# Cross-attention of a decoder layer: the context's layer norm folded into the key and value weights, the context loaded turned

## The reference, cut to what matters

```
xn = layernorm(x)   * gamma + beta          # over 256 features, eps 1e-5
cn = layernorm(ctx) * gamma + beta          # 361 rows
q, k, v = xn @ Wq, cn @ Wk, cn @ Wv         # 16 heads of 16
q, k = rope(q), rope(k)                     # even/odd halves of 8, tables of cos and sin by position
p = softmax(q @ k.T / 4 + temporal_bias)    # the bias as a factor exp(bias) on the exponentials
y = p @ v
o = y @ Wout + b_out ; g = sigmoid(o @ Wgate + b_gate) ; out = layernorm(mix of o and x by g)
```

## Time and profile before

| what | value |
|---|---|
| median of three runs | 2173.53 us (2172.13 to 2187.19) |
| the profiled execution: its own time | 2181.74 us |
| its span, first to last instruction | 2180.0 us |
| mean granted TensorE clock | 0.896 |
| busy: PE, PEld, DVE, ACT, POOL | 1913.7, 1446.5, 1430.0, 991.3, 1000.9 us |
| the stage in this execution | about 1233 to 1988 us |

### The profile page before, as it was taken

One profiled execution on the slowest core, in us unless ns is written; L12 is line 12 of the kernel. 1 busy time (PEld: TensorE's weight loads), 2 busy tenths in 40 slices (PEclk: granted clock), 3 DMA queues, 4 the chain that ended last, 5 costly groups with the idle time before them and its releaser, 6 DMA issues. The chain is left out here.

```text
span 2180.0 us, 60448 instructions
## 1 busy us (share of the span) xinstructions
PE 1913.7 (88%) x21298; PEld 1446.5 (66%) x21298; DVE 1430.0 (66%) x3458; ACT 991.3 (45%) x1977; POOL 1000.9 (46%) x1042
## 2 busy tenths in 40 slices
PE   7999979997998499759999689999999999984665
PEld 4677758886888277548888456666676767652332
DVE  3777756775877444336766457777676767655998
ACT  2555534441111043323444245555555555534897
POOL 1333331221777443355553136565656565642443
PEclk8999989997999599968999689999999999985556
DMA  5311118992211399443331111110101010001111
GB/s 181 107 36 34 34 52 289 331 330 80 54 54 49 114 299 296 127 133 100 96 97 39 46 31 31 32 35 28 37 25 37 25 37 25 21 9 31 58 57 42
DMA packets 157099, 192.81 MB, mean 88 GB/s; under 512 B 27971, under 2 KB 140614, under 8 KB 157013
## 3 DMA queue, kind: packets, MB, share of 16 engines
q1 hardware_dynamic: 146741, 189.07, 27.7%
q0 software_dynamic: 10272, 2.62, 0.6%
HBM read 140.78 MB, written 77.51 MB: 100 GB/s over the span
## 5 line engine op out<-in xcount | busy, mean ns | idle before, releaser
L2964 DVE TENSOR_REDUCE xa_kq<-xa_A 100x4 f32<-100x1444 f32 x128 | 212.7, 1661 | 158.1 <-PE xa_A L2633 158.1
L2792 ACT ACTIVATE xa_prob<-xa_A 121x1600 f32<-121x1600 f32 x96 | 144.5, 1505 | 235.3 <-PE xa_A L2660 235.3
L2867 POOL TENSOR_TENSOR xa_prob<-xa_prob,xa_exp_bias 121x1600 f32<-121x1600 f32 x64 | 228.5, 3571 | 40.8 <-ACT xa_prob L2792 40.8
L1429 POOL DMA_INDIRECT slot_rows<-rt_x_again,rt_slot_u x150 | 154.7, 1031 | 67.5 <-issue 62.7
L2892 POOL TENSOR_TENSOR xa_o_rstd<-xa_o_var,xa_power 100x1 f32<-100x1 f32 x32 | 17.8, 555 | 241.4 <-DVE xa_o_var L3004 241.4
L2660 PEld LDWEIGHTS xa_A<-xa_q2T,xa_kqT 17*121 17x121 f32 x3072 | 92.3, 184 | 46.0 <-issue 29.0
L2633 PE MATMUL xa_A<-xa_kqT 16*100 16x361 f32 x1024 | 113.0, 511 | 6.8 <-ACT xa_prob L2792 6.8
L1675 POOL DMA_INDIRECT contrib<-ex_y,ex_place_u x64 | 62.2, 973 | 120.4 <-ACT ex_y L1727 107.9
L2660 PE MATMUL xa_A<-xa_q2T,xa_kqT 17*121 17x100 f32 x3072 | 108.5, 278 | 4.8 <-DVE xa_kq L2964 4.2
L2577 PE MATMUL xa_C<-xa_wk,xa_rows_T 128*121 128x256 f32 x384 | 103.8, 409 | 1.7 <-ACT xa_rows_T L2772 1.7
L2577 PE MATMUL xa_C<-xa_wv,xa_rows_T 128*121 128x256 f32 x384 | 101.3, 401 | 0.0
(11 more groups left out here) (352 smaller groups left out, 5150.8 us busy)
## 6 DMA issues: line engine op xcount, KB each, us to landing
ex_w<-in_w13T SPq DMA_DIRECT2D x64, 352.0 KB
contrib<-xs_zero SPq DMA_DIRECT2D x30, 640.0 KB
la_rows<-contrib SPq DMA_DIRECT2D x16, 1200.0 KB
xs_ctxT<-in_ctxT SPq DMA_DIRECT2D x32, 512.0 KB
xa_rows_t<-in_ctx SPq DMA_DIRECT2D x96, 121.0 KB
ex_w<-in_w2T SPq DMA_DIRECT2D x64, 176.0 KB
slot_rows<-xs_zero SPq DMA_DIRECT2D x32, 272.0 KB
ex_x_t<-slot_rows SPq DMA_DIRECT2D x64, 136.0 KB, 5.7
```

The source lines that it names most:

```text
L1429: nc.gpsimd.indirect_dma_start(slot_rows, bass.IndirectOffsetOnAxis(slot_u[:, k, n:n + 1], 0), x_again[:, k, :], None, bounds_check=SLOTS ...
L2792: nc.scalar.activation(prob[:, n, :].rearrange("p (h a) -> p h a", h=HPG), A[:ROWS, :, 0:G * T], ACT.Exp, scale=EXP_SCALE).then_inc(exp_re ...
L2867: nc.gpsimd.tensor_tensor(chunk, chunk, exp_bias[:, n, :].unsqueeze(1).to_broadcast([ROWS, HEADS, T]), ALU.mult).then_inc(biased, 1)
L2964: nc.vector.tensor_reduce(kq[:T, k, NCH, 4 * j:4 * j + 4, DH:DH + 1].rearrange("p h o -> p (h o)"), A[:T, :, 0:src_len], axis=AXIS_X, op=A ...
```

## The change

1. **Context loaded turned.** The host lays the context out a second time (`ctx_cols`, features on partitions). SP loads it straight into `rows_T` (`columns`, one DMA of 128x2x361, 370 KB), after the values of the batch two before (`v_done`). The row loads stay, for the moments. `normalise`, `turn_rows` and `rows_out` do the queries' lot alone: one activation for four, 2 transposes for 8, evictions of 121 columns for 482. `keys_first` waits for the DMA, not for `rows_out`.
2. **Norm folded into weights.** `wkv` is gamma times the weights, less the mean over the features, so the context's mean drops out of keys and values. Made once at the start of the stage, with the constant shares of beta: `k_bias` (the rotated share of the keys) and an addition to `bo` and `less` (the share of the values, taken to the output side).
3. **The roots.** The context's 1/sqrt(var) is multiplied into the rotation tables (POOL, two small instructions in `raise_power`, `cos_r` and `sin_r`) and into the scale of the values' evictions on ACT (`values_first` becomes two instructions).
4. **A new step on DVE.** `add_key_bias` adds `k_bias` to `kq` (121x768, in place) after `finish_rope`; `turn_kq` 0 waits for it (`kq_ready`) and no longer for `summed`.
5. **Moved.** POOL's `raise_power` goes from ahead of `finish_rope` to the end of the body, ACT's `normalise` from the middle to the end. The clearing of `kq` goes from DVE to POOL.

The diff, with the declarations and waits of the setup left out:

```diff
+                def columns(b):
+                    k = b[1] % 2
+                    sp.wait_ge(v_done, at(b, 2, -2))
+                    sp.dma_start(rows_T[:, k, :, 0:src_len], w["ctx_cols"][b[0] * 2 + b[1]]).then_inc(cols_loaded[k], 16)
...
                 def turn_rows(b):
                     k = b[1] % 2
                     pe.wait_ge(normed, at(b, 1, 1))
+                    pe.wait_ge(kqT_ready, at(later(b, -1), G, G))
                     for c in range(KC):
-                        if c == 0:
-                            pe.wait_ge(kqT_ready, at(later(b, -1), G, G))
-                        else:
-                            pe.wait_ge(dg_ready, at(later(b, -4), 1, 1))
-                        for n in range(LOTS):
-                            o = n * STEP if n < NCH else src_len
-                            last = nc.tensor.transpose(C[1 + c][:, o:o + ROWS], rows_n[:, k, n, c * P:(c + 1) * P], ident[:ROWS, :ROWS])
-                        last.then_inc(turned, 1)
+                        last = nc.tensor.transpose(C[1][:, c * ROWS:(c + 1) * ROWS], x_n[:, k, c * P:(c + 1) * P], ident[:ROWS, :ROWS])
+                    last.then_inc(turned, 1)
...
                 def keys_first(b):
-                    pe.wait_ge(rowsT_ready, at(b, KC, KC))
+                    pe.wait_ge(cols_loaded[b[1] % 2], loads_of(b, 1))
...
                 def turn_kq(b, j):
                     k = b[1] % 2
                     if j == 0:
-                        pe.wait_ge(summed, at(b, 1, 1))
+                        pe.wait_ge(kq_ready, at(b, 1, 1))
...
                 def values_first(b):
...
-                    nc.scalar.activation(v1[:, k, 0:2, :, 0:DH].rearrange("p n h d -> p (n h) d"),
-                                         C[0][:ROWS, :].rearrange("p (a d) -> p a d", d=DH), ACT.Copy).then_inc(v_ready, 1)
+                    act.wait_ge(rstd_ready, at(b, 1, 1))
+                    for n in range(2):
+                        last = nc.scalar.activation(v1[:, k, n, :, 0:DH], C[0][:ROWS, n * D:(n + 1) * D].rearrange("p (a d) -> p a d", d=DH),
+                                                    ACT.Copy, scale=rstd[:, k, n:n + 1])
+                    last.then_inc(v_ready, 1)
...
                 def raise_power(b):
...
+                    pool.wait_ge(roped, at(later(b, -2), 2, 2))
+                    for scaled, table in ((cos_r, cos), (sin_r, sin)):
+                        last = nc.gpsimd.tensor_tensor(scaled[:, k, 0:NCH, :], table[:, 0:NCH, :],
+                                                       rstd[:, k, 0:NCH].unsqueeze(2).to_broadcast([ROWS, NCH, H2]), ALU.mult)
+                    last.then_inc(tables_ready, 1)
...
+                def add_key_bias(b):
+                    k = b[1] % 2
+                    dve.wait_ge(summed, at(b, 1, 1))
+                    keys = kq[:, k, 0:NCH, :, 0:DH]
+                    nc.vector.tensor_tensor(keys, keys, k_bias[:], ALU.add).then_inc(kq_ready, 1)
```

At the start of the stage, the folding (DVE's and PE's parts):

```diff
+                for m, wm in enumerate((wk, wv)):
+                    for c in range(KC):
+                        nc.vector.tensor_scalar(wkv[:, c, m * D:(m + 1) * D], wm[:, c, :], gamma[:, c:c + 1], None, ALU.mult).then_inc(gained, 1)
...
+                for c in range(KC):
+                    last = nc.tensor.matmul(A[:, 0, :], part[:], wkv[:, c, :], start=(c == 0), stop=(c == KC - 1))
+                last.then_inc(meaned, 1)
...
+                dve.wait_ge(meaned, 1)
+                for c in range(KC):
+                    nc.vector.tensor_tensor(wkv[:, c, :], wkv[:, c, :], A[:, 0, :], ALU.subtract).then_inc(folded, 1)
```

More of the change, by code:

```diff
@@ L2477, in cross_attention @@
         fused, fused_sb, wide_ready = s.sem("fused_in_psum"), s.sem("fused_in_sbuf"), s.sem("wide_ready")
+        gained, part_set, meaned, folded, steps_done = (s.sem(n) for n in ("gained", "part_set", "meaned", "folded", "steps_done"))
+        cols_loaded = [s.sem(f"cols_loaded{k}") for k in range(2)]
+        tables_ready, tables_set, kq_ready = (s.sem(n) for n in ("tables_ready", "tables_set", "kq_ready"))
         loaded = [s.sem(f"loaded{k}") for k in range(2)]
@@ L2530, in _ @@
                 rows((0, 0))
+                columns((0, 0))
                 rows((0, 1))
@@ L2539, in body @@
                         store(later(b, -2))
+                    if has(3):
+                        columns(later(b, 3))
                 periods(sp, NB, FIRST, LAST, REACH, body)
@@ L2558, in _ @@
                 pe.wait_ge(fused_sb, 1)
+                for c in range(KC):
+                    last = nc.tensor.matmul(A[:T, 3, :], bvT[:, c, :], wog[:, c, :], start=(c == 0), stop=(c == KC - 1))
+                last.then_inc(fused, 1)
+                pe.wait_ge(folded, KC)
+                pe.wait_ge(fused_sb, 2)
                 def turn_rows(b):
@@ L2717, in body @@
                     if has(-1):
-                        turn_out(later(b, -1), has(2))
+                        turn_out(later(b, -1))
                     if has(1):
@@ L2782, in normalise @@
                     act.wait_ge(shift_ready, at(b, 1, 1))
-                    act.wait_ge(turned, at(later(b, -2), KC, KC))
-                    for n in range(LOTS):
-                        last = nc.scalar.activation(rows_n[:, k, n, :], rows_t[:, k, n, :], ACT.Identity, scale=rstd[:, n:n + 1],
-                                                    bias=shift[:, n:n + 1])
-                    last.then_inc(normed, 1)
+                    act.wait_ge(turned, at(later(b, -2), 1, 1))
+                    nc.scalar.activation(x_n[:, k, :], rows_t[:, k, NCH, :], ACT.Identity, scale=rstd[:, k, NCH:LOTS],
+                                         bias=shift[:]).then_inc(normed, 1)
                 def exponential(b, n):
@@ L2836, in body @@
                         y_out(later(b, -1))
-                    if has(3):
-                        normalise(later(b, 3))
                     if has(0):
@@ L2849, in body @@
                             kq_out(later(b, 2), j)
+                    if has(3):
+                        normalise(later(b, 3))
                 normalise((0, 0))
@@ L2905, in body @@
                         apply_bias(b, 0)
-                    if has(3):
-                        raise_power(later(b, 3))
                     if has(2):
@@ L2912, in body @@
                         residual(b)
+                    if has(3):
+                        raise_power(later(b, 3))
+                pool.wait_ge(w_in, W_ALL)
                 raise_power((0, 0))
-                pool.wait_ge(w_in, W_ALL)
                 periods(pool, NB, FIRST, LAST, REACH, body)
@@ L3032, in body @@
                         maxima(later(b, 1), 2)
+                    if has(2):
+                        add_key_bias(later(b, 2))
                     if has(-1):
```

106 lines of the change are left out of this document (74 added, 32 removed).

## The result

| | before | after |
|---|---|---|
| median of the runs, us | 2174.22 (4 runs, 2172.13 to 2187.19) | 2209.56 (4 runs, 2200.34 to 2212.17) |
| ratio of the two | | 1.0145, 95% interval 1.0107 to 1.0182 |
| profiled execution, us | 2181.74 | 2208.52 |
| period (store to store), us | 21.57 | 22.40 |
| first memset of the stage to the first of the next stage, us | 755.8 | 782.5 |

The changed kernel is 1.45% slower, by medians 35 us, with 23 to 40 us in the interval. The two profiled executions differ by 26.8 us, and the stage accounts for 26.7 of them; the sum of the prediction was 27.6.

What follows compares the result with a forecast made beforehand. It took two equal chains, PE's work and DVE's three instructions, to bound a period's last third. 18.6 us for periods plus 9 for the start gave + 27.6, 2201 us against the median 2173.53; range 2176 to 2217.

Steps and rivals of the forecast that it cites:

- The addition: DVE's addition of k_bias stands until POOL's instruction ends, so `turn_kq` 0 waits and `score` 3 starts 0.61 us late.
- The transposes: Six of eight row transposes go, 0.69 us of PE in a period's last third; only 0.09 us comes back.
- two equal chains: In a period's last third, PE's work and DVE's three instructions, both behind `score` 3, run equally long; DVE's slack 0.09 us.
- the predicted wait: PE idle 0.6 us ahead of `score_turned` 0, released by DVE's maximum 0.
- ACT ... I cost it at nothing.: ACT's normalising, now at the body's end, costs nothing: the transposes behind it have 0.69 us of room.
- A period: Each loop period grows by 0.61 + 0.10 - 0.09 = 0.62 us, times 30: 18.6 us, bounds 12 to 27.
- The start: At the stage's start, first transposes come 10 to 15.5 us later; net + 9 us, bounds + 2 to + 13.
- my full-clock case: At the stage's start with PE at full clock, first transposes come near 1257, for 1246.44 before.
- No waiting: Rival: the addition runs beside POOL's instruction in DVE's hole, no change, 2180 us; chance 0.15.
- the transposes count: Rival: PE, not DVE, holds up `score_turned` 0, so 0.69 us per period comes back, 2162 us; chance 0.08.
- the late DMA: Rival: PE waits for the context's DMA at `keys_first` in each period, over 2215 us; chance 0.03.
- POOL wins again: Rival: the addition also waits for `residual`, or the tables hold DVE's bias 0.5 us; 2216 to 2240 us; chance 0.13.

Runs made afterwards that it cites:

- a2: The changed kernel with DVE's addition of k_bias cut to one chunk, 121x256 for 121x768: period 21.87 us.
- b1: The kernel before with six of the eight row transposes left out, evictions kept: period 21.52 us, for 21.57 before.
- b3: The kernel before with six of eight row transposes left out and the third bias moved from DVE to POOL: period 21.46 us.
- a7: a5 with the third bias on POOL, the keys' fourth turn moved behind `score` 0, the row transposes behind `attend` 2: period 21.24 us.
- a4: The changed kernel with POOL's power and `shift` back ahead of `finish_rope`, table products left at the end, ACT's normalise mid-body again: period 22.14 us.
- a5: a4 in which POOL's second apply_bias also waits for the addition: period 21.54 us.
- a8: The changed kernel with the clearing of `kq` moved from POOL to DVE, behind its four gamma products: period 22.40 us, stage 779.1 us for 782.5.
- a3: The changed kernel with POOL's second apply_bias made to wait for the addition, nothing left out: period 26.69 us.

## Why the prediction was right

- **The addition.** Right in mechanism and in size: DVE holds still until POOL's instruction ends (a2), it ends 0.82 us after it, PE's `turn_kq` 0 is released by it. `score` 3 was to be 0.61 late; it was 0.60 on average, and without the addition the period falls by 0.60.
- **The transposes.** Right: 0.09 us was to come back, b1 gives 0.06. The reason was incomplete. I saw two equal chains; b3 shows a third, so that even a shorter DVE would have opened only 0.11. Their own price was too high as well: I took 6/8 of the group, 0.69 us, but a group of two fills 0.30 (b1) or 0.36 (a7), so six fewer are 0.62 or 0.56. It did not matter here, since hardly any of it could come back.
- **"The prediction is wrong at its root if PE, not DVE, still ends the wait before `score_turned` 0."** In the changed kernel this sign did appear: PE's own order, late by its wait for x_n, comes to `score_turned` 0 after maximum 0 is over, and its row shows no idle time. The extra delay of the next point covered the predicted wait. With that delay removed (a4) the wait stands there, 0.50 us for the 0.6 forecast, and DVE ends it, so the root holds.
- **"ACT ... I cost it at nothing."** This step failed. Its room of 0.69 us was counted from ACT's side; what came late was its input, POOL's `shift`. I had put POOL's table products next to DVE's bias and priced that meeting as 0.10 us *on DVE*. It fell the other way: DVE kept the operands, and POOL's `shift`, of one element, was held for 2.6 us. The term is 0.26 (a4) where 0.10 stood, and it sits on PE's row transposes, not on maximum 0. My times were not at fault. They had the power end near 1517.1 and the bias start at 1517.81, so `shift` would start 0.7 us ahead of the bias, as it then did (0.76), and by its 0.2 us be over long before. What I lacked is that the bias keeps POOL out before its recorded start, and no row of before shows that.
- **A period**: + 0.62 predicted, + 0.83 measured. The parts are 0.60 for the addition and 0.26 for the late `shift`, less 0.06 from the transposes, and 0.02 at `score_turned` 1 that I cannot name; with both waits removed the period is 0.03 below that of before (a5). The factor was too large in turn: 25 of the intervals had the full 0.83, and the four after them were 1.6 us shorter together. 18.6 predicted, 19.1 measured, with two errors that cancel: the closeness is luck.
- **The start.** 10 to 15.5 us to the first transposes; it was 8.0. The order of the steps was right, and the clearing of `kq` was worth its 3.5 us (a8), though it came ahead of the products and not between them. What I had left open was the clock. PE reached full speed during the folding: the window 1247 to 1250 us has 1.00, and the product of wg with woT took 1.89 us where it took 3.75 before. That is my full-clock case, which had 10.6, and the 2.6 us below it are not taken apart here. Net + 7.4 for + 9.
- **The number.** The sum (+ 27.6) hit the difference of the profiled executions (26.8), with the start 1.6 too dear and the periods 0.5 too cheap. I then took 8.2 us off, since the execution profiled before was that far above its median. The one profiled after was 1.0 below its own, so the median moved by 35 us and not by 28, and 2201 was 8.6 us short of 2209.56.
- **The rivals.** "No waiting" is refuted by a2 and by the addition's 3.64 us in the changed kernel, "the transposes count" by b1, the late DMA by PE's rows, in which no wait for it stands. "POOL wins again" named a time close to the result (2216 and up), but POOL's `residual` did not come ahead of the addition. Its other half, a second meeting with DVE's bias, is what happened, at 0.26 us and with the engines exchanged.

What stays open: that a7 ends at 21.24 rather than 21.0 for want of room on PE was read from PE's rows, not tested. How long before its start the bias keeps POOL out is not known either: the rows show it for starts of POOL 0.5 to 0.8 us behind the start of DVE's instruction before it.

## What to carry to other kernels

When a cheap two-operand addition in SBUF goes to DVE, price it by what POOL runs at that moment, and then follow POOL's queue to its end: each delay moves POOL's next small instruction towards DVE's next long one. Leave room ahead of the long one's recorded start as well: here a POOL instruction that would have been over 0.57 us before it was held to its end. Before counting freed time on the busiest engine, look for the chains that end at the same point; PE was 99% busy here, and six transposes less gave 0.06 of 0.62 us.

## What was not expected of the hardware

- An instruction of 121x1 on POOL lasted 2.62 us because DVE's multiplication by the bias, 121x1600, was next in DVE's queue and then ran. It was held from 0.76 us before that instruction's recorded start. The hold works in both directions, and the length of the one that waits does not matter: 3.64 us for 768 elements, 3.17 for 256. The one that waits ends 0.13 to 0.15 us short of its own length after the other: the additions, `shift` and, in a3, `twice` all do.
- A wait of 2.5 us on PE (a3) was followed by a granted clock of 0.53 over the next 6 us, most of it at the 1.2 GHz level, for 1.00 before: eight matmuls of 256 columns took 3.77 us for 1.99. A wait of 0.6 us in each period (after) left the clock at 1.00 from 1320 us on. The period grew by 5.1 us, twice the wait: on average 2.35 us more from `score` 0 to `score_turned` 0, where the wait is, and 2.56 more from there to `score` 1, where the clock is low.
